# Linear attention with an FFN on one core: block of q ahead of the turn back, an earlier o transpose and a joint gate product in ten tiles, later low parts on GpSimd

## What is computed

```python
x = x + attention(layernorm(x))
x = x + ffn(layernorm(x))

# attention, 16 heads of 32, chunks of 128 rows
q, k, v = silu(x @ Wq), silu(x @ Wk), x @ Wv          # then rotated q, k
scores = einsum('bthd,bshd->bhts', qi, ki) * D        # D: decay mask
o = scores @ vi + (qi * decay_q) @ S                  # S: running state
S = lam_C * S + (ki * decay_k).T @ vi
gate = x @ Wg1 @ Wg2
o = rmsnorm_by_head(o * sigmoid(gate)) * norm_weight
return o @ Wo

# ffn, 4-bit weights with a scale for every 32 of them
inter = gelu(x @ Wg.T) * (x @ Wu.T)
return inter @ Wd.T
```

## Time and profile before

| what | us |
|---|---|
| median of three runs | 1290.05 |
| lowest and highest run | 1288.67, 1290.23 |
| profiled execution, its own time | 1288.75 |
| span of the profiled execution (first to last instruction) | 1286.7 |
| TensorE busy in the span | 1270.3 |
| VectorE busy in the span | 917.0 |
| granted TensorE clock | 1.00 |

### The profile page before, as it was taken

The page is one execution under the profiler, slowest core; times in us unless marked ns, Lnnn a source line. Parts: engine busy times, 40 slices in busy tenths (PEclk is TensorE's granted clock), DMA queues, the critical chain, the costliest instruction groups (busy, mean ns, idle before and its releaser), DMA issues.

```text
span 1286.7 us, 20699 instructions
## 1 busy us (share of the span) xinstructions
PE 1270.3 (99%) x7376; PEld 1043.5 (81%) x7376; DVE 917.0 (71%) x1594; ACT 475.2 (37%) x799; POOL 435.2 (34%) x360
## 2 busy tenths in 40 slices
PE   9999999998999999999999999999999999999998
PEld 6888888887788888888888888888888888888887
DVE  7878788788867667676767676767767666767665
ACT  5433434434433333333333433333333333333421
POOL 2434455564442322223132324133232324232400
PEclk9999999999999999999999999999999999999999
DMA  9000000000001000010000000001001000000003
GB/s 326 12 2 1 19 17 2 2 1 2 25 25 33 17 33 27 22 33 28 29 24 24 24 24 24 33 16 33 24 24 33 24 33 24 24 24 24 24 13 119
DMA packets 21778, 40.23 MB, mean 31 GB/s; under 512 B 2660, under 2 KB 2916, under 8 KB 21604
## 3 DMA queue, kind: packets, MB, share of 16 engines
q1 hardware_dynamic: 21060, 39.47, 9.4%
q10 hardware_dynamic: 672, 0.13, 0.1%
HBM read 35.40 MB, written 4.19 MB: 31 GB/s over the span
## 4 chain that ended last, share of the span: by engine, by line
PE 93%; DVE 2%; POOL 1%; ACT 1%; issue 1%; POOLq 0%; DVEq 0%; ACTq 0%
PE bank L1351 16%; PE bank L1354 15%; PE bank L1353 15%; PE bank L1197 13%; PE bank L1199 13%; PE bank L1198 13%; PE bank L1211 2%; PE bank L1291 1%; PE bank L1310 1%; PE bank L1300 1%; PE bank L1343 1%; PE bank L1331 1%; PE bank L1258 0%; ACT xg L394 0%; PE bank L1257 0%
## 5 line engine op out<-in xcount | busy, mean ns | idle before, releaser
L883 DVE TENSOR_TENSOR acc<-acc,bank 128x512 f32<-128x512 f32 x248 | 169.3, 683 | 129.4 <-PE bank L1199 129.3
L1197 PE MATMUL bank<-wdh,hh 128*128 128x512 f32 x512 | 199.3, 389 | 0.0
L1199 PE MATMUL bank<-wdh,hl 128*128 128x512 f32 x512 | 199.2, 389 | 0.0
L1198 PE MATMUL bank<-wdl,hh 128*128 128x512 f32 x512 | 199.2, 389 | 0.0
L1351 PE MATMUL bank<-xoh,wgh 128*128 128x512 f32 x448 | 175.9, 393 | 0.6 <-DVE cxa L891 0.6
L1351 PE MATMUL bank<-xoh,wuh 128*128 128x512 f32 x448 | 175.1, 391 | 0.7 <-ACT cxa L482 0.7
L1354 PE MATMUL bank<-xoh,wgl 128*128 128x512 f32 x448 | 174.5, 390 | 0.0
L1354 PE MATMUL bank<-xoh,wul 128*128 128x512 f32 x448 | 174.3, 389 | 0.0
L1353 PE MATMUL bank<-xol,wuh 128*128 128x512 f32 x448 | 174.3, 389 | 0.0
L1353 PE MATMUL bank<-xol,wgh 128*128 128x512 f32 x448 | 174.3, 389 | 0.0
L899 DVE TENSOR_TENSOR hl<-hx,hh 128x512 fp32r<-128x512 f32 x128 | 113.5, 887 | 51.4 <-ACT hh L489 51.0
(11 more groups left out here) (163 smaller groups left out, 2285.7 us busy)
## 6 DMA issues: line engine op xcount, KB each, us to landing
stg<-packed_dram SPq DMA_DIRECT2D x48, 256.0 KB, 2.5
stg<-scales_dram SPq DMA_DIRECT2D x48, 256.0 KB
out_dram<-acc SPq DMA_DIRECT2D x16, 256.0 KB, 2.0
acc<-x_dram SPq DMA_DIRECT2D x3, 1024.0 KB, 15.0
w_in<-wq_dram SPq DMA_DIRECT2D x2, 512.0 KB, 5.2
w_in<-wk_dram SPq DMA_DIRECT2D x2, 512.0 KB, 6.9
w_in<-wv_dram SPq DMA_DIRECT2D x2, 512.0 KB, 8.6
w_in<-wo_dram SPq DMA_DIRECT2D x2, 512.0 KB, 11.2
```

The lines of the kernel that those rows point to most:

```text
L883: V.tensor_tensor(row, row, BY[j % 2][:], ALU.add).then_inc(y_add, 1)
L1197: pe.matmul(dst, w_h, x_h, start=start, stop=False)
L1198: pe.matmul(dst, w_h, x_l, start=False, stop=False)
L1199: return pe.matmul(dst, w_l, x_h, start=False, stop=stop)
```

## The change

Four things are done together. A list `TURNED_EARLY` names ten tiles.

1. In tiles with c < 3, `o_back(t)` moves behind `q_part(0)`.
2. In the ten tiles, `o_transpose(t - 1)` moves ahead of `v_project(t + 1)`. ScalarE's and VectorE's split of its result, `ot_hi_` and `ot_lo_`, move forward too, and VectorE's `gate_low` moves back behind `xt_lo_`.
3. For the tile after each of them (`together(u)`), `gate1` takes the high and the low part of x in one matmul of 256 columns; they now lie in one buffer `xt`. The two halves of the result are added: ScalarE copies the first (`gate_copy`, 128 x 128), VectorE adds the second (`sum_gate`, 128 x 128). The scores wait for that sum and no longer for `g_lo`.
4. GpSimd's `unit_lo` moves behind `scaled` and `decay_k_`, and in tiles 7 and 9 it waits for `xg_done` of the tile.

```diff
+TURNED_EARLY = (2, 3, 4, 6, 7, 8, 9, 10, 11, 12)
...
+        def together(u):
+            return u - 1 in TURNED_EARLY
...
 # ScalarE
+            def gate_copy(t):
+                act.wait_ge(g1_ps, t + 1)
+                act.wait_ge(gate_sum, sums(t))
+                A(gs[:, 0, :], BS[3][:, 0:P], ACT.Copy).then_inc(g1_sb, 1)
...
                 silu_qk(t + 1)
+                if together(t + 1):
+                    gate_copy(t + 1)
+                if t in TURNED_EARLY:
+                    ot_hi_(t - 1)
                 gate_low(t + 1)
...
 # VectorE
+            def sum_gate(t):
+                dve.wait_ge(g1_sb, sums(t) + 1)
+                dve.wait_ge(g_hi, t)
+                V.tensor_tensor(gs[:, 1, :], gs[:, 0, :], BS[3][:, P:2 * P], ALU.add
+                                ).then_inc(gate_sum, 1)
...
                 decayed_q(t)
+                if t in TURNED_EARLY:
+                    sum_gate(t + 1)
+                    ot_lo_(t - 1)
+                    rope_of(b, c, t + 1, (c + 1) % CHUNKS)
+                    masked(t)
+                    xt_lo_(t + 2)
+                    gate_low(t + 1)
+                    add_x1(t - 1)
...
 # GpSimd
-                unit_lo(t, 0)
                 if 1 <= c < CHUNKS - 1:
                     scaled(b, c)
-                unit_lo(t, 1)
                 if c + 1 < CHUNKS - 1:
                     decay_k_(b, c + 1, t + 1)
+                if t in UNIT_PARTS[:2]:
+                    pool.wait_ge(xg_done, t + 1)
+                unit_lo(t, 0)
+                unit_lo(t, 1)
...
 # TensorE
+                    ins = pe.matmul(BS[3][:, 0:2 * P].rearrange("p (a t) -> p a t", a=2),
+                                    g1s[:, k, :, :].rearrange("p r d -> p (r d)"), x[:, :, k, :],
+                                    start=(k == 0), stop=(k == KT - 1))
...
                 gate1(t + 1)
+                if t in TURNED_EARLY:
+                    o_transpose(t - 1)
...
                 v_project(t + 1)
-                if not at_start(b, c):
+                if not at_start(b, c) and t not in TURNED_EARLY:
                     o_transpose(t - 1)
...
-                if c < CHUNKS - 1:
-                    o_back(t)
                 q_ready(t + 2)
                 for k in range(KT):
-                    if c == CHUNKS - 1 and k == 2:
+                    if k == (1 if c < CHUNKS - 1 else 2):
                         o_back(t)
                     q_part(k)
```

More of the change, by code:

```diff
@@ L250, in near_end, with sums @@
             return isinstance(b, int) and b * CHUNKS + c + ahead >= TILES
+        def together(u):
+            return u - 1 in TURNED_EARLY
+        def sums(u):
+            return sum(together(v) for v in range(u))
         def at_start(b, c):
@@ L463, in tile @@
                 if not at_start(b, c):
-                    ot_hi_(t - 1)
+                    if t not in TURNED_EARLY:
+                        ot_hi_(t - 1)
                     xt_hi_(t + 2)
@@ L844, in tile @@
                 decayed_q(t)
[L845 to L848, removed]
[L849 to L852 removed]
+                if t in TURNED_EARLY:
+                    sum_gate(t + 1)
+                    ot_lo_(t - 1)
+                    rope_of(b, c, t + 1, (c + 1) % CHUNKS)
[3 more added lines that the diff above has]
+                    add_x1(t - 1)
+                else:
+                    gate_low(t + 1)
+                    if at_start(b, c):
+                        xt_lo_(2)
+                    rope_of(b, c, t + 1, (c + 1) % CHUNKS)
+                    if not at_start(b, c):
+                        ot_lo_(t - 1)
+                    masked(t)
+                if not at_start(b, c) and t not in TURNED_EARLY:
                     xt_lo_(t + 2)
@@ L1253, in gate1 @@
                 pe.wait_ge(gate_tanh, t)
-                xh, xl = x_of(t)
+                x = ot if t == 1 else xt
                 for k in range(KT):
[L1256 to L1259, removed]
+                    if not together(t):
+                        g1 = g1s[:, k, :, :].rearrange("p r d -> p (r d)")
+                        pe.matmul(BS[3][:, 0:P], g1, x[:, 0, k, :], start=(k == 0), stop=False)
+                        ins = pe.matmul(BS[3][:, 0:P], g1, x[:, 1, k, :], start=False,
+                                        stop=(k == KT - 1))
+                        continue
+                    ins = pe.matmul(BS[3][:, 0:2 * P].rearrange("p (a t) -> p a t", a=2),
+                                    g1s[:, k, :, :].rearrange("p r d -> p (r d)"), x[:, :, k, :],
+                                    start=(k == 0), stop=(k == KT - 1))
                 ins.then_inc(g1_ps, 1)
@@ L1414, in tile @@
                     pe.wait_ge(xg_done, t)
-                pe.wait_ge(g_lo, t + 2)
+                if together(t + 1):
+                    pe.wait_ge(gate_sum, sums(t + 2))
+                else:
+                    pe.wait_ge(g_lo, t + 2)
                 for g in range(KT):
@@ L1469, in passage @@
                 pe.wait_ge(xg_done, s)
-                pe.wait_ge(g_lo, t + 1)
+                if together(t):
+                    pe.wait_ge(gate_sum, sums(t + 1))
+                else:
+                    pe.wait_ge(g_lo, t + 1)
                 for g in range(KT):
```

53 lines of the change are left out of this document (32 added, 21 removed).

## The result

The changed kernel takes **1293.12 us** (median of 11 runs, 1292.56 to 1294.99), the kernel before, timed with it, 1288.82. The ratio is 1.0032, with a 95% interval from 1.0024 to 1.0040: slower by 4 us. The forecast was 1290.1, no change, and its range ended at 1293.1; the time lies on that end, a fiftieth of a microsecond beyond it. The profiled execution took 1293.9 with a span of 1291.9, which is 5.2 us more than before.

The account below looks back on a forecast made before the run. TensorE, busy 99% of the span, was taken as the bound. -3.7 - 3.1 + 0.3 + 3.1 + 3.4 = 0.0 us on 1288.75, set 1.3 higher at the three-run median: 1290.1 us, range 1283.3 to 1293.1.

Parts of the forecast that it names:

- Joint gate product: gate1 in ten tiles: four matmuls of 256 columns at 0.12 us each save 0.37 us a tile, 3.7 us.
- rival (b): At L1309 the joint product saves nothing, four matmuls of 256 columns taking 0.21 us each: 1293.1 us; chance 0.10.
- o_back: Moved behind q_part(0), it loses its wait for ScalarE's copy: 0.35 us in each of nine tiles, 3.1 us saved.
- The small waits in tiles 2, 6 and 9: At the early o_transpose, distances within 0.1 us of zero where gated or normed is late: 0.3 us charged for all three.
- The chain behind the low parts: gated to on_done in tiles 7 and 9, held by GpSimd: TensorE waits 3.1 us in tile 8, 3.4 in tile 10.
- the pair: GpSimd's two low-part instructions in tiles 7 and 9 hold Newton operations, the first and third: 2.4 us late.
- rb: GpSimd's two instructions of the next tile may each stop one operation, 0 to 2 us; 1.0 us taken.
- unit_bits is freed: In tile 7 the low parts no longer collide with unit_bits: gated(7) 1.8 us earlier by this, at about 165.6.
- rival (c): unit_bits stays held, gated as late as before in both tiles, waits 1.8 us longer each: 1293.7 us; chance 0.08.
- Rival (a): The low parts don't hold the chain from gated to on_done; both waits vanish, gains stand: 1283.6 us; chance 0.32.
- the two long waits: TensorE's waits for on_done at the early o_transpose: 3.1 us in tile 8 (2.1 to 4.1), 3.4 in tile 10 (2.4 to 4.4).

Follow-up runs that it names:

- the second experiment: The changed kernel with 19 more matmuls of 512 columns just ahead of o_transpose in tiles 8 and 10, where TensorE waited: 1290.03 us, ratio 1.0009.

## Why the prediction was right or wrong

**Joint gate product: right.** L1309 takes 0.12 us from start to start (79.11 to 79.58 for four), where 0.12 was taken between bounds of 0.11 and 0.23; eight matmuls of 128 columns took 0.85:

```profile
79.11 0.63 PE L1309 MATMUL bank<-xt,g1s 128*128 128x256 f32 x4
79.58 0.60 PE L1258 MATMUL bank<-idt,sq 128*128 128x128 f32 x4
```

So 0.38 us a tile were saved, and rival (b) fell. The Trainium skill's figures for the issue of matmuls alone ("TensorE: Matmul & The Clock Gate", "Back-to-back issue gap") would have made this worth nothing. The runs decide: 0.106 us for 128 columns and 0.12 for 256. In the trace every one of these matmuls has a weight load of its own, and before the change the loads, too, started 0.11 us apart; that the load sets the pace and hides the second 128 columns fits this, but was not tested by itself.

**o_back: right, a little small.** 0.35 us a tile was worked out from the distances in tile 3 and 4; 0.40 to 0.44 came, the whole of the wait and no cost for the one more interruption. Each turned tile gained some 0.1 us more, whose cause was not traced, and the gains, net of the small waits, were 8.1 us, not 6.5.

**The small waits in tiles 2, 6 and 9** (0.3 us) did not come; tile 12 has 0.47 instead, and o_transpose(13) in the passage waits 0.85 where it had waited 0.47.

**The chain behind the low parts: the right mechanism, one term too small.** The prediction counted from gated(7) to on_done(7) 5.1 + 2.4 (the pair) + 1.0 (rb), 8.5 us. It was 9.73. The pair's term held: 0.64 + 1.87 = 2.5, though the two operations held were the first and the second, not the first and the third. rb's did not: L658 lost 1.1 and L655 1.0, together 2.1, the upper end of the 0 to 2 that stood there. I had taken one hold of two because before, rb had met only one operation. But that was because the chain had ended: the one it met was the last. Where small operations still follow each other, every piece of rb finds one. In tiles 8 and 10 the waits were thus 4.46, past the upper bounds of 4.1 and 4.4.

**unit_bits is freed: right.** Its operations in tile 7 keep 0.41 to 0.69 us. Of rival (c) nothing came in tile 9 but one of 1.22 us (0.8 late). Times on the trace's scale such as 165.6 for gated(7) (its own terms add up to 165.7) were off, though, since the prediction added only that tile's own gains to the times of before; the kernel was already 3.8 to 4.3 us ahead there, and gated(7) came at 161.90. The distances within the tile held: TensorE reached the new place 5.33 us behind gated(7), where 5.4 was worked out. Rival (a), that the low parts don't hold the chain, is dead.

**The clock: not in the prediction at all.** This is the step that failed. After "waits 3.1 us" the text went on as if TensorE then worked as before. It does not: about 2.2 us were lost behind each of two waits of 4.46 us, shown by the windows and, as the edit that keeps TensorE busy gives 2.1 and 2.0 back, by the second experiment. The kernel before had no wait near that length and its clock stood at full in every slice, so no row showed the price. But the prediction put a wait of 3 us where there had been none longer than 1.5, and took TensorE's speed behind it as given, without a bound for it in the range. What a wait of the forecast's 3.1 us would have cost is open: waits of 2.3 to 2.4 us left the clock at 1.00 in the one trace that has them, and one of 3.83 us lost 1.4.

By size, in the profiled execution: the gains, net of the small waits, were 1.6 us more than forecast (8.1 for 6.5), the two long waits 2.4 us more (8.9 for 6.5), the clock 4.4, together 5.2 us where 0.0 was forecast. By the medians it is 4.3. The forecast of no change failed by the last two, and that the time came within 0.02 us of the range's end is luck, twice over: that end was the price of rival (b), which did not happen, and the forecast had been set 1.3 us above the profiled execution, on a median of three runs that eleven runs put at 1288.82 and not at 1290.05.

## What to carry to other kernels

When a consumer on the critical engine is moved ahead of the work that covered its producer, count the holds instruction by instruction: each GpSimd instruction that overlapped this chain of small VectorE operations cost it up to the whole of that instruction, and moving it elsewhere only helps where VectorE has slack. GpSimd work that is due at a fixed distance behind a TensorE stretch (rb here) can be made to wait for the end of the chain; this one wait was worth 4 us by the medians here, 2.9 of them traced. And a wait of TensorE has to be priced with what the clock does afterwards: in the profiled execution 4.5 us of waiting cost 6.7.

## What the runs showed of the hardware that was not expected

- An operation of 128 x 16 that takes 0.17 us took 2.04 us beside a GpSimd instruction of 2.1 us, and 1.17 to 1.29 beside one of 1.25. The hold ends with the instruction, within 0.05 us, whatever the size of what is held. It also catches operations with one tensor input in SBUF and a scalar (L651, L652), and a gate_low of 32 x 128 (0.30 us alone, 2.08 held). A reduction from SBUF (L733, 0.69 us) was not held, nor, in the kernel before, two operations beside rb that read one operand from PSUM (L805, 0.68 us at 174.03, and L685, 0.30 at 174.74).
- TensorE had stopped at 167.2 us; its clock fell to 0.50 between 169 and 170 and was back at 1.00 at 177, when it had worked since 171.7. In the run with the low parts behind normed it had stopped at 184.2, and the clock fell only between 187 and 188. A matmul of 512 columns then took 0.43 us from start to start, against 0.23.
- Waits of 2.3 to 2.4 us kept the clock in the one trace that has them. In the passage two idle stretches of 1.17 and 1.02 us with little work between them were followed by a stretch at 0.50 in some executions and not in others. The changed kernel's profile has none there:

```profile
306.00:308.00 2.00, 1.35 (x11) 1.00 0.00 0
```

That of the kernel with the filled waits, which is there 4 us earlier, has one:

```profile
302.00:304.00 2.00, 2.00 (x12) 0.51 0.00 0
```

What decides it there stays open.
